# Norm, GeGLU and ternary down projection on one core: input preparation of later blocks spread over more steps, peak steps in two parts, GpSimd's long sums in short pieces

## The chip, the cores and the metric

One core of one Trainium2 chip runs the whole program. The metric is the device time of one execution in microseconds, taken as the median of several executions. Times inside the trace are microseconds from the start of the span of one profiled execution.

## What is computed

```
scale = cond @ norm_w.T + 1.0
ms = jnp.mean(x * x, axis=-1, keepdims=True)
h = x * (scale[:, None, :] * jax.lax.rsqrt(ms + EPS))
u = h @ up_w.T
val, gate = jnp.split(u, 2, axis=-1)
h = val * jax.nn.gelu(gate, approximate=False)
hq = act_quant(h)          # a row's values times 127 / row peak, rounded
wq = weight_quant(down_w)  # -1, 0 or 1, times one scale
y = hq @ wq.T
return y + x
```

x has 4 x 1024 rows of 512; up_w is 4096 x 512, down_w 512 x 2048, all float32. Float32 products are made of three float16 ones (high by high, low by high, high by low part).

## The kernel before

The 4096 rows are cut into 8 blocks of 512 tokens (b = 0 to 7), and the 2048 hidden columns into 16 tiles of 128 (j = 0 to 15). One step n = 16 b + j makes one tile of hidden values for one block. There is no scheduler: every engine has a program written out by hand, a loop over n whose body tests j against numbers, and the engines keep pace by semaphores. An engine does its own list strictly in order.

From block 2 on, a step of the up projection is a Strassen-like scheme with seven products of half tiles. On TensorE, step n runs `first_pair(n)` (12 matmuls), `third(n-1)` (6), `gates(n-1)` (12), `second(n)` (6) and `fourth(n-1)` (6). Between them stand small jobs of the other engines:

- ScalarE: `copies(n)` (lines 926 and 929) takes both halves of the first pair out of PSUM, and `second(n)` waits for it; then `absolute(n-2)` (949) and `gelu(n-1)` (942), then the step's extras.
- VectorE: `hidden(n-2)` (1317), `second_val(n-1)` (1305, which `fourth(n-1)` waits for), in steps 3 to 10 two `quantized` tiles of the block before (1398), `peak_of(n-2)` (1330), `residual` where there is one (1412), `seed_gate(n)` (1300, which `third(n)` waits for), then the step's extras.

The extras prepare block b + 1 while block b is multiplied: `norm` (1266, four per block) scales the input tile xt by the row factors; `difference` makes the sums of the scheme (XT1 into ta, XT2 into tb, XT3 in place, XN4 into ta); ScalarE's `high` (984) rounds each of seven operands to float16, and VectorE's `low` (1295) makes what is left. The row factors come from ScalarE's squares and VectorE's `rsqrt` (12 tiny instructions, lines 1239 to 1253); SyncE stores them in HBM and loads them again spread over all partitions (`store_rs`, `load_rs`), and ScalarE's `order_rs` (972) turns them into the order that `norm` reads.

For blocks 2 to 6 the row peaks are found on VectorE in the block after: `turn_peaks` (1337, 1339) at step 1 and `spread_peaks` (1347 to 1365) at step 2; the `quantized` tiles from step 3 on need its last instruction. The down projection of blocks 2 to 6 is also made of seven products, with sums on GpSimd: `down_terms` once, after step 38 (1154 to 1159), `sum_tokens` per pair of tiles (1170 to 1173), and `sum_last` (1180) after the first products of a pair of row groups, at steps 11 and 15. `row_dequant` (1388) prepares the factors for the output.

Of the kernel before, what the change touches and what calls it, by code (L numbers as in the profile page):

```python
# [8 lines left out]
ALU = mybir.AluOpType  # L9
# [36 lines left out]
def bass_cond_norm_geglu_bitlinear(  # L46
# [86 lines left out]


    V_FIRST = 2

    def h_home(b, j):
        return J + j if j < 2 and b % 2 == 1 else j
# [30 lines left out]
    with ExitStack() as ctx:  # L169
# [207 lines left out]
            return {1: 6, 2: J - 1}.get(c, (c - 1) * J)  # L377

        def rsqrt_at(c):
            return {1: 5, 2: 14, 3: J + 14, 4: 2 * J + 13}.get(c, (c - 2) * J + 11)  # L380

        def rs_away(c):

            return 1 if c == RS_DRAM else 2

        def squares_at(c, i):
            return {1: 1, 2: 9, 3: J - 1, 4: 2 * J + 9}.get(c, (c - 2) * J + 6) + i

        def xs_tile(c, i):

# [244 lines left out]
        def _(pe):  # L635
# [159 lines left out]
            def d_pair(b, p):  # L795

                x = d_index(b)
                if x == 0 and p == 0:
                    pe.wait_ge(dt_step, 4)
# [12 lines left out]

            def d_gates(b, p):
                d_product(d_high(0), q_parts[:, :, 1, 0, p, :], d_b[:, :, 1, 0, :])
                pe.wait_ge(ds4_ready, 2 * d_index(b) + p + 1)
# [106 lines left out]
        def _(act):  # L922
# [105 lines left out]
            for n in range(NJ + 2):  # L1028
# [24 lines left out]
                    if n == SUM_AT[k]:  # L1053
                        sum_high(k)
                if 1 <= b < NB - 1:
                    if j == 2:
                        high(b + 1, XB11)
                        high(b + 1, XT1)
                    if j == (2 if b < 3 else 5):
                        high(b + 1, XT2)  # L1060
                    if j == (2 if b < 3 else 8):
                        high(b + 1, XT3)
                    if j == (3 if b < 3 else 9):
                        high(b + 1, XB21)
                        high(b + 1, XB22)
                    if j == (3 if b < 3 else 11):
                        high(b + 1, XN4)
# [14 lines left out]
        def _(pool):  # L1082
# [66 lines left out]

            def down_terms():  # L1150

                b11, b12, b21, b22 = [d_b[:, :, i // 2, i % 2, :] for i in range(4)]
                pool.wait_ge(ws_ready, J)
                pool.tensor_tensor(d_t[:, 0], b12, b11, ALU.subtract, saturate=False).then_inc(dt_step, 1)
                pool.wait_ge(dt_step, 1)
                pool.tensor_tensor(d_t[:, 1], b22, d_t[:, 0], ALU.subtract, saturate=False).then_inc(dt_step, 1)
                pool.tensor_tensor(d_t[:, 2], b22, b12, ALU.subtract, saturate=False).then_inc(dt_step, 1)
                pool.wait_ge(dt_step, 2)
                pool.tensor_tensor(d_t[:, 3], b21, d_t[:, 1], ALU.subtract, saturate=False).then_inc(dt_step, 1)

            def sum_tokens(b, k):

# [12 lines left out]
            def sum_last(b, p):  # L1175

                x = d_index(b)
                pool.wait_ge(dp_ready, 2 * x + p + 1)
                pool.wait_ge(ds_step, 3 * NK * (x + 1))
                pool.tensor_tensor(q_parts[:, :, 0, 0, p, :], q_parts[:, :, 1, 0, p, :], d_s2[:, p],  # L1180
                                   ALU.subtract).then_inc(ds4_ready, 1)

            down_terms()
            for b in D_SEVEN:
# [6 lines left out]
        def _(dve):  # L1191
# [150 lines left out]
            def spread_peaks(b):  # L1342
# [15 lines left out]
                dve.tensor_scalar(scale_all[0:Q, :], row_inv, QMAX * STEP16, None, ALU.mult).then_inc(peak_step, 1)  # L1358
                dve.wait_ge(peak_step, base + 8)
# [3 lines left out]
                dve.wait_ge(xn_ready, min(b + 3, NB) * KT)  # L1363
# [89 lines left out]
            for n in range(NJ + 2):  # L1453
# [69 lines left out]
                if 1 <= b < NB - 1:  # L1523
                    if j == (0 if b == 1 else 1):
                        for kt in range(KT):
                            norm(b + 1, kt)
# [5 lines left out]
                if 1 <= b < NB - 1:  # L1532
                    if j == 2:
                        difference(b + 1, XT1)
                    if j == (2 if b < 3 else 4):
                        difference(b + 1, XT2)
                        low(b + 1, XB11)
                    if j == (2 if b < 3 else 7):
                        difference(b + 1, XT3)
                        low(b + 1, XT1)  # L1540
                    if j == (2 if b < 3 else 10):
                        difference(b + 1, XN4)
                    if j == 15:
                        for k in (XT2, XT3, XB21, XB22, XN4):
                            low(b + 1, k)
                for c in range(1, NB):
                    if n == rsqrt_at(c):
# [53 lines left out]
```

## Time and profile before

| | |
|---|---|
| time, median of 3 runs | 748.75 us (748.67 to 749.0) |
| profiled execution, its own time | 745.14 us |
| its span | 743.3 us |
| TensorE busy | 726.3 us, 98% of the span |
| VectorE busy | 548.1 us, 74% |
| ScalarE busy | 343.7 us, 46% |
| GpSimd busy | 236.3 us, 32% |
| share of TensorE in the chain that ended last | 89% |
| granted TensorE clock | 1.00 |

A share of busy time is an average over the span. A matmul's length in the trace is modelled and overlaps the next one, so the distance from one start to the next is what says how fast TensorE goes.

### The profile page before, as it was taken

Reading aid. Unit: us, or ns where it says so; the run is one execution under the profiler, and the core shown is the slowest. Engines: PE = TensorE matmul, PEld = TensorE weight load, DVE = VectorE, ACT = ScalarE, POOL = GpSimd, SP = SyncE. Lnnn points to the kernel's source line nnn. Section 1 sums busy time; section 2 is a strip of 40 time slices with the busy share of each in tenths; the row PEclk is TensorE's granted clock in tenths of the full one; section 3 lists DMA queues with packets and bytes.
Section 4 is the critical chain, followed back from the end, with each engine's and each line's share of the span. In section 5 each row is a group of like instructions: output and inputs, shape, how many; then the busy total and the mean of one; then the engine's idle time right before and its main releaser. Section 6 shows DMA issues by size and latency. Waiting matters only on the chain.

```text
span 743.3 us, 14907 instructions
## 1 busy us (share of the span) xinstructions
PE 726.3 (98%) x5722; PEld 557.9 (75%) x5722; DVE 548.1 (74%) x1024; ACT 343.7 (46%) x680; POOL 236.3 (32%) x286
## 2 busy tenths in 40 slices
PE   6999999999999999999999999899998999999998
PEld 6544444444688887888888888788887888888874
DVE  5567777975989666886689857897579955687357
ACT  5789766543365533463325534355334443334330
POOL 1211477876325300452105511154012530033100
PEclk9999999999999999999999999999999999999999
DMA  8877583847645454442545325353253324273202
GB/s 327 299 267 240 182 285 118 280 164 250 221 138 145 148 187 123 155 143 76 171 134 165 121 89 188 104 185 100 83 195 122 111 80 127 81 236 102 74 29 85
DMA packets 44567, 117.63 MB, mean 158 GB/s; under 512 B 5584, under 2 KB 5840, under 8 KB 43344
## 3 DMA queue, kind: packets, MB, share of 16 engines
q1 hardware_dynamic: 44496, 116.68, 47.9%
q8 instruction: 45, 0.74, 0.4%
q14 instruction: 26, 0.21, 0.1%
HBM read 99.88 MB, written 16.79 MB: 157 GB/s over the span
## 4 chain that ended last, share of the span: by engine, by line
PE 89%; DVE 5%; issue 3%; ACT 1%; DMA 1%; POOL 0%; DVEq 0%; SPq 0%; POOLq 0%
PE ps_v L649 13%; PE ps_v L651 13%; PE ps_v L650 13%; PE ps_y L785 6%; PE ps_g L651 5%; PE ps_g L649 5%; PE ps_g L650 5%; PE ps_y L778 5%; PE ps_v L667 4%; PE ps_g L667 4%; PE ps_v L669 4%; PE ps_g L669 4%; PE ps_v L668 4%; PE ps_g L668 4%; PE ps_v L907 1%
## 5 line engine op out<-in xcount | busy, mean ns | idle before, releaser
L649 PE MATMUL ps_v<-x_hi,w_hi 128*128 128x256 f16 x968 | 263.9, 273 | 7.7 <-ACT p L929 6.3
L650 PE MATMUL ps_v<-x_lo,w_hi 128*128 128x256 f16 x968 | 263.8, 273 | 0.0
L651 PE MATMUL ps_v<-x_hi,w_lo 128*128 128x256 f16 x968 | 263.8, 273 | 0.0
L926 ACT COPY ps_g<-ps_v 128x256 f32<-128x256 f32 x96 | 34.3, 357 | 185.6 <-PE ps_v L651 185.6
L949 ACT ACTIVATE g<-h 128x512 f32<-128x512 f32 x128 | 81.2, 634 | 72.0 <-DVE h L1317 72.0
L942 ACT ACTIVATE g<-ps_g,w_unscale 128x512 f32<-128x512 f32 x128 | 87.1, 681 | 58.1 <-PE ps_g L651 53.6
L649 PEld LDWEIGHTS ps_v<-x_hi,w_hi 128*128 128x128 f16 x968 | 94.7, 98 | 21.2 <-ACT p L929 7.1
L1170 POOL TENSOR_TENSOR sums<-q 128x256 f16<-128x256 f16 (+1 forms) x40 | 40.0, 1001 | 214.9 <-DVE q L1398 214.9
L649 PE MATMUL ps_g<-x_hi,w_hi 128*128 128x256 f16 x392 | 106.8, 273 | 0.1
L650 PE MATMUL ps_g<-x_lo,w_hi 128*128 128x256 f16 x392 | 106.8, 273 | 0.0
L651 PE MATMUL ps_g<-x_hi,w_lo 128*128 128x256 f16 x392 | 106.8, 273 | 0.0
L1330 DVE TENSOR_TENSOR h_max<-g,h_max 128x512 f32<-128x512 f32 x120 | 88.7, 739 | 20.7 <-ACT g L949 16.7
L650 PEld LDWEIGHTS ps_v<-x_lo,w_hi 128*128 128x128 f16 x968 | 94.7, 98 | 11.6
L651 PEld LDWEIGHTS ps_v<-x_hi,w_lo 128*128 128x128 f16 x968 | 94.7, 98 | 11.0
L1305 DVE TENSOR_TENSOR ps_v<-ps_v,p 128x256 f32<-128x256 f32 x96 | 41.1, 428 | 78.5 <-PE ps_v L651 78.2
L1317 DVE SCALAR_TENSOR_TENSOR h<-ps_v,h_unscale,g 128x512 f32<-128x512 f32 x128 | 95.1, 743 | 4.3 <-PE ps_v L669 1.4
L1398 DVE TENSOR_TENSOR q<-h,ps_m 128x512 f16<-128x512 f32 x112 | 71.3, 676 | 0.0
L1300 DVE TENSOR_TENSOR ps_g<-ps_v,p 128x256 f32<-128x256 f32 x96 | 41.0, 427 | 35.7 <-PE ps_v L651 35.5
L1180 POOL TENSOR_TENSOR q<-q,sums 128x1024 f16<-128x1024 f16 x9 | 20.1, 2229 | 113.0 <-PE ps_y L785 113.0
L667 PE MATMUL ps_g<-x_hi,w_hi 128*128 128x512 f16 x124 | 47.0, 379 | 0.0
L668 PE MATMUL ps_g<-x_lo,w_hi 128*128 128x512 f16 x124 | 47.0, 379 | 0.0
L669 PE MATMUL ps_g<-x_hi,w_lo 128*128 128x512 f16 x124 | 47.0, 379 | 0.0
(153 smaller groups left out, 1161.9 us busy)
## 6 DMA issues: line engine op xcount, KB each, us to landing
w_lo<-w_lo_dram SPq DMA_DIRECT2D x96, 448.0 KB, 3.2
q<-in_up_t_dram SPq DMA_DIRECT2D x16, 512.0 KB, 5.4
xt<-in_x_cols_dram SPq DMA_DIRECT2D x8, 1024.0 KB, 5.0
res<-in_x_rows_dram SPq DMA_DIRECT2D x26, 256.0 KB, 4.4
out_dram<-res SPq DMA_DIRECT2D x26, 256.0 KB, 4.1
xs<-in_x_rows_dram SPq DMA_DIRECT2D x22, 256.0 KB, 3.9
w_lo_dram<-w_lo SPq DMA_DIRECT2D x16, 256.0 KB, 4.7
dw<-in_down_t_dram SPq DMA_DIRECT2D x8, 512.0 KB, 6.5
```

The costliest lines, as they stand in the source:

```text
L649: pe.matmul(to, w_hi[:, wh:wh + P], hi, start=start and kt == 0, stop=False, skip_group_check=True)
L650: pe.matmul(to, w_hi[:, wh:wh + P], lo, start=False, stop=False, skip_group_check=True)
L651: last = pe.matmul(to, w_lo[:, wl:wl + P], hi, start=False, stop=(kt == 1), skip_group_check=True)
L667: pe.matmul(bank, w_hi[:, wh:wh + P], hi, start=start and kt == 0, stop=False)
L668: pe.matmul(bank, w_hi[:, wh:wh + P], lo, start=False, stop=False)
L669: last = pe.matmul(bank, w_lo[:, wl:wl + P], hi, start=False, stop=not start and kt == 1)
L785: last = pe.matmul(to, left[:, k, :], right[:, k, :], start=start and k == 0, stop=k == NK - 1, skip_group_check=True)
L942: act.activation(g[:, n % 3, :], ps_g[:, n % NG, :], ACT.Gelu, scale=w_unscale[:, n % J:n % J + 1]).then_inc(g_ready, 1)
L949: act.activation(g[:, n % 3, :], h[:, at:at + TB], ACT.Abs).then_inc(h_abs_ready, 1)
L1317: dve.scalar_tensor_tensor(out=h[:, at:at + TB], in0=ps_v[:, n % NV, :], scalar=h_unscale[:, j:j + 1], in1=g[:, n % 3, :], op0=ALU.mult, o ...
L1330: dve.tensor_tensor(h_max[:], g[:, n % 3, :], h_max[:], ALU.max).then_inc(h_max_ready, 1)
L1398: dve.tensor_tensor(to[:, j * TB:(j + 1) * TB], h[:, at:at + TB], ps_m[:], ALU.mult).then_inc(q_ready, 1)
```

## The change

Inputs of blocks 4 to 7 (made during blocks 3 to 6) are prepared on a new timetable; blocks 2 and 3 keep theirs. The four `norm` go from step 1 to steps 3, 4, 6, 7, one each. `difference` goes from steps 2, 4, 7, 10 to 5, 8, 11, 11. `high` goes from steps 2, 2, 5, 8, 9, 9, 11 to 5, 6, 9, 12, 12, 12, 12, and `low` from 4, 7 and five of them in step 15 to 9, 10, 12, 13, 13, 14, 15. `rsqrt` of blocks 5 to 7 goes from step 11 to 14 (for block 4 from 13 to 14), and the store, load and `order_rs` behind it come 3 steps later (2 for block 4), so that `order_rs` falls on step 2. The squares of blocks 5 to 7 come 3 steps later too. `spread_peaks` is cut in two: its first seven instructions, `gather_peaks`, follow `turn_peaks` in step 1, and the last four stay in step 2. `row_dequant` of blocks 2 to 6 goes from step 5 to 11. `down_terms` is made in 8 parts (32 instructions of 256 columns in place of 4 of 2048), and each `sum_last` in 4 (256 columns in place of 1024). TensorE's list of instructions is the same, with the counts that it waits for changed.

```diff
+    NORM_AT = (3, 4, 6, 7)
+    T_AT = {XT1: 5, XT2: 8, XT3: 11, XN4: 11}
+    HIGH_AT = {XB11: 5, XT1: 6, XT2: 9, XT3: 12, XB21: 12, XB22: 12, XN4: 12}
+    LOW_AT = {XB11: 9, XT1: 10, XT2: 12, XT3: 13, XB21: 13, XB22: 14, XN4: 15}
...
         def rsqrt_at(c):
-            return {1: 5, 2: 14, 3: J + 14, 4: 2 * J + 13}.get(c, (c - 2) * J + 11)
+            return {1: 5, 2: 14, 3: J + 14}.get(c, (c - 2) * J + 14)
...
         def squares_at(c, i):
-            return {1: 1, 2: 9, 3: J - 1, 4: 2 * J + 9}.get(c, (c - 2) * J + 6) + i
+            return {1: 1, 2: 9, 3: J - 1}.get(c, (c - 2) * J + 9) + i
...
-                pool.tensor_tensor(d_t[:, 0], b12, b11, ALU.subtract, saturate=False).then_inc(dt_step, 1)
...
+                for k in range(NK):
+                    part = slice(k, k + 1)
+                    b11, b12, b21, b22 = [d_b[:, part, i // 2, i % 2, :] for i in range(4)]
+                    t1, t2, t3, t4 = [d_t[:, i, part] for i in range(4)]
+                    pool.tensor_tensor(t1, b12, b11, ALU.subtract, saturate=False).then_inc(dt_step, 1)
...
-                pool.tensor_tensor(q_parts[:, :, 0, 0, p, :], q_parts[:, :, 1, 0, p, :], d_s2[:, p],
-                                   ALU.subtract).then_inc(ds4_ready, 1)
+                for k in range(0, NK, 2):
+                    pool.tensor_tensor(q_parts[:, k:k + 2, 0, 0, p, :], q_parts[:, k:k + 2, 1, 0, p, :], d_s2[:, p, k:k + 2],
+                                       ALU.subtract).then_inc(ds4_ready, 1)
...
+                if 3 <= b < NB - 1 and j in NORM_AT:
+                    norm(b + 1, NORM_AT.index(j))
...
-                if 1 <= b < NB and j == 5:
+                if 1 <= b < NB and j == (11 if by_vector(b - 1) else 5):
                     row_dequant(b - 1)
...
+                if 1 <= b < NB and j == 1 and by_vector(b - 1):
+                    gather_peaks(b - 1)
...
+                if 3 <= b < NB - 1:
+                    for k in (XT1, XT2, XT3, XN4):
+                        if j == T_AT[k]:
+                            difference(b + 1, k)
+                    for k in made(b + 1):
+                        if j == LOW_AT[k]:
                             low(b + 1, k)
```

VectorE at step 2 of block 4, from `seed_gate` on, before. The 32x16 instructions are `spread_peaks`, `ta<-xt` is the difference XT1, and `h<-ps_v` opens step 3:

```order
L1300 TENSOR_TENSOR ps_g<-ps_v,p 128x256
L1412 SCALAR_TENSOR_TENSOR res<-ps_y,dequant,res 128x512
L1347 COPY tb<-tb 32x16 x3
L1350 TENSOR_REDUCE row_peak<-tb 32x16
L1353 TENSOR_SCALAR row_peak<-row_peak 32x16
L1355 RECIPROCAL tb<-row_peak 32x16
L1358 TENSOR_SCALAR tb<-tb 32x16
L1361 COPY tb<-tb 32x16 x3
L1365 STREAM_TRANSPOSE ps_m<-tb 128x512
L1275 TENSOR_TENSOR ta<-xt 128x512
L1317 SCALAR_TENSOR_TENSOR h<-ps_v,h_unscale,g 128x512
L1305 TENSOR_TENSOR ps_v<-ps_v,p 128x256
```

The same place after:

```order
L1302 TENSOR_TENSOR ps_g<-ps_v,p 128x256
L1418 SCALAR_TENSOR_TENSOR res<-ps_y,dequant,res 128x512
L1367 COPY tb<-tb 32x16 x3
L1371 STREAM_TRANSPOSE ps_m<-tb 128x512
L1319 SCALAR_TENSOR_TENSOR h<-ps_v,h_unscale,g 128x512
L1307 TENSOR_TENSOR ps_v<-ps_v,p 128x256
```

Seven of the eleven small instructions have gone to step 1, where four `norm` have left, and the difference to step 5.

ScalarE at step 2 of block 4 before: `copies`, `absolute`, `gelu`, two `high` (the second reads ta), and step 3:

```order
L926 COPY ps_g<-ps_v 128x256
L929 COPY p<-ps_v 128x256
L949 ACTIVATE g<-h 128x512
L942 ACTIVATE g<-ps_g,w_unscale 128x512
L984 CAST x_hi<-xt 128x512
L984 CAST x_hi<-ta 128x512
L926 COPY ps_g<-ps_v 128x256
L929 COPY p<-ps_v 128x256
```

And after:

```order
L933 COPY ps_g<-ps_v 128x256
L936 COPY p<-ps_v 128x256
L956 ACTIVATE g<-h 128x512
L949 ACTIVATE g<-ps_g,w_unscale 128x512
L979 COPY xs<-xs 128x512
L933 COPY ps_g<-ps_v 128x256
L936 COPY p<-ps_v 128x256
```

Both `high` have left step 2, and `order_rs` (`xs<-xs`) has come.

VectorE from `seed_gate` of step 14 of block 3, before: the second residual, then step 15 at once:

```order
L1300 TENSOR_TENSOR ps_g<-ps_v,p 128x256
L1412 SCALAR_TENSOR_TENSOR res<-ps_y,dequant,res 128x512
L1317 SCALAR_TENSOR_TENSOR h<-ps_v,h_unscale,g 128x512
L1305 TENSOR_TENSOR ps_v<-ps_v,p 128x256
L1330 TENSOR_TENSOR h_max<-g,h_max 128x512
```

After, with a `low` and the `rsqrt` (12 instructions of 128x4; the middle ones are left out) in front of step 15:

```order
L1302 TENSOR_TENSOR ps_g<-ps_v,p 128x256
L1418 SCALAR_TENSOR_TENSOR res<-ps_y,dequant,res 128x512
L1297 TENSOR_TENSOR x_lo<-xt,x_hi 128x512
L1241 TENSOR_SCALAR ms<-sumsq 128x4
...
L1255 SCALAR_TENSOR_TENSOR rs<-rs_t,rs 128x4
L1319 SCALAR_TENSOR_TENSOR h<-ps_v,h_unscale,g 128x512
L1307 TENSOR_TENSOR ps_v<-ps_v,p 128x256
```

Thirteen instructions more now stand between `seed_gate(62)` and `second_val(62)`; the same holds in blocks 4 and 5.

## Rows read from the trace of the kernel before

**Rows 1.** The page, parts 1 and 4: busy time, and the chain's shares

```profile
PE 726.3 (98%) x5722; PEld 557.9 (75%) x5722; DVE 548.1 (74%) x1024; ACT 343.7 (46%) x680; POOL 236.3 (32%) x286
...
PE 89%; DVE 5%; issue 3%; ACT 1%; DMA 1%; POOL 0%; DVEq 0%; SPq 0%; POOLq 0%
```

**Rows 2.** Waits, whole span: waiter <- releaser: us in total, times, longest

```profile
PE ps_v L649 <- ACT p L929: 6.3, 3, 2.1
...
PE ps_v L649 <- DVE ps_g L1300: 0.7, 1, 0.7
...
PE ps_v L649 <- DVE ps_v L1305: 0.6, 1, 0.6
```

**Rows 3.** Timeline of TensorE, 388.1 to 390.9: start, length, instruction, [idle before <- releaser]

```profile
388.25 0.27 PE L651 MATMUL ps_g<-x_hi,w_lo 128*128 128x256 f16 x1
390.61 0.28 PE L649 MATMUL ps_v<-x_hi,w_hi 128*128 128x256 f16 x1 [2.09 <-ACT p L929]
```

**Rows 4.** Timeline of ScalarE, 381 to 392.5

```profile
389.36 0.62 ACT L984 CAST x_hi<-ta 128x512 f16<-128x512 f32 x1 [4.79 <-DVE ta L1275]
...
390.19 0.37 ACT L929 COPY p<-ps_v 128x256 f32<-128x256 f32 x1
```

**Rows 5.** Timeline of VectorE, 376 to 391.5

```profile
378.10 2.73 DVE L1266 SCALAR_TENSOR_TENSOR xt<-xt,cs,xs 128x512 f32<-128x512 f32 x4
...
385.75 0.56 DVE L1347 COPY tb<-tb 32x16 f32<-32x16 f32 x3
...
387.29 0.56 DVE L1361 COPY tb<-tb 32x16 f32<-32x16 f32 x3
...
388.64 0.69 DVE L1275 TENSOR_TENSOR ta<-xt 128x512 f32<-128x512 f32 x1
```

**Rows 6.** Timelines of TensorE, GpSimd and VectorE, 228 to 249

```profile
236.55 0.28 PE L649 MATMUL ps_v<-x_hi,w_hi 128*128 128x256 f16 x1 [0.73 <-DVE ps_g L1300]
...
231.77 3.83 POOL L1154 TENSOR_TENSOR dw<-dw 128x2048 fp8e4<-128x2048 fp8e4 x1 [22.06 <-DVE xs L1226]
...
233.79 2.36 DVE L1330 TENSOR_TENSOR h_max<-g,h_max 128x512 f32<-128x512 f32 x1
236.07 0.42 DVE L1300 TENSOR_TENSOR ps_g<-ps_v,p 128x256 f32<-128x256 f32 x1
```

**Rows 7.** Timelines of TensorE and VectorE in the last block, 652 to 654

```profile
653.33 0.28 PE L649 MATMUL ps_v<-x_hi,w_hi 128*128 128x256 f16 x1 [0.61 <-DVE ps_v L1305]
...
652.85 0.42 DVE L1305 TENSOR_TENSOR ps_v<-ps_v,p 128x256 f32<-128x256 f32 x1
```

**Rows 8.** Timelines of VectorE and TensorE, steps 14 and 15 of block 3

```profile
360.52 0.74 DVE L1412 SCALAR_TENSOR_TENSOR res<-ps_y,dequant,res 128x512 f32<-128x512 f32 x1
361.18 0.74 DVE L1317 SCALAR_TENSOR_TENSOR h<-ps_v,h_unscale,g 128x512 f32<-128x512 f32 x1
362.80 0.43 DVE L1305 TENSOR_TENSOR ps_v<-ps_v,p 128x256 f32<-128x256 f32 x1 [0.88 <-PE ps_v L651]
...
364.56 0.27 PE L649 MATMUL ps_v<-x_hi,w_hi 128*128 128x256 f16 x1
```

**Rows 9.** Timeline of VectorE, 262 to 265: first of the `rsqrt`, and what follows it

```profile
262.65 0.16 DVE L1239 TENSOR_SCALAR ms<-sumsq 128x4 f32<-128x4 f32 x1
...
264.94 0.75 DVE L1317 SCALAR_TENSOR_TENSOR h<-ps_v,h_unscale,g 128x512 f32<-128x512 f32 x1
```

**Rows 10.** Timeline of VectorE, 308 to 311, extras of step 4, block 3

```profile
308.72 0.82 DVE L1281 TENSOR_TENSOR tb<-xt,ta 128x512 f32<-128x512 f32 x1
309.46 1.15 DVE L1295 TENSOR_TENSOR x_lo<-xt,x_hi 128x512 f16<-128x512 f32 x1
```

**Rows 11.** Groups of GpSimd by line and form: count | busy, mean ns | idle before

```profile
L1170 POOL TENSOR_TENSOR sums<-q 128x256 f16<-128x256 f16 x32 | 33.6, 1050 | 174.3 <-DVE q L1398 174.3
...
L1180 POOL TENSOR_TENSOR q<-q,sums 128x1024 f16<-128x1024 f16 x9 | 20.1, 2229 | 113.0 <-PE ps_y L785 113.0
```

**Rows 12.** DMA issues by line: count, size, median us from issue to landing

```profile
xs<-rs_dram SPq DMA_DIRECT2D x4, 256.0 KB, 3.7
```

More of the change, by code:

```diff
@@ L135, in bass_cond_norm_geglu_bitlinear @@
     V_FIRST = 2
+    NORM_AT = (3, 4, 6, 7)
+    T_AT = {XT1: 5, XT2: 8, XT3: 11, XN4: 11}
+    HIGH_AT = {XB11: 5, XT1: 6, XT2: 9, XT3: 12, XB21: 12, XB22: 12, XN4: 12}
+    LOW_AT = {XB11: 9, XT1: 10, XT2: 12, XT3: 13, XB21: 13, XB22: 14, XN4: 15}
+    HIGH_EARLY = {XB11: 2, XT1: 2, XT2: 2, XT3: 2, XB21: 3, XB22: 3, XN4: 3}
     def h_home(b, j):
@@ L379, in rsqrt_at @@
         def rsqrt_at(c):
-            return {1: 5, 2: 14, 3: J + 14, 4: 2 * J + 13}.get(c, (c - 2) * J + 11)
+            return {1: 5, 2: 14, 3: J + 14}.get(c, (c - 2) * J + 14)
         def rs_away(c):
-            return 1 if c == RS_DRAM else 2
+            return 2
         def squares_at(c, i):
-            return {1: 1, 2: 9, 3: J - 1, 4: 2 * J + 9}.get(c, (c - 2) * J + 6) + i
+            return {1: 1, 2: 9, 3: J - 1}.get(c, (c - 2) * J + 9) + i
         def xs_tile(c, i):
@@ L798, in d_pair @@
                 if x == 0 and p == 0:
-                    pe.wait_ge(dt_step, 4)
+                    pe.wait_ge(dt_step, 4 * NK)
                 pe.wait_ge(ds_step, 3 * NK * (x + 1))
@@ L814, in d_gates @@
                 d_product(d_high(0), q_parts[:, :, 1, 0, p, :], d_b[:, :, 1, 0, :])
[L815 removed]
+                pe.wait_ge(ds4_ready, (2 * d_index(b) + p + 1) * NK // 2)
                 d_product(d_high(1), q_parts[:, :, 0, 0, p, :], d_b[:, :, 1, 1, :]).then_inc(y_ready, 1)
@@ L1055, in _ @@
                 if 1 <= b < NB - 1:
[L1056 to L1067, printed above, removed]
+                    for k in made(b + 1):
+                        if j == (HIGH_EARLY if b < 3 else HIGH_AT)[k]:
+                            high(b + 1, k)
                 for c in range(1, NB):
@@ L1150, in down_terms @@
             def down_terms():
-                b11, b12, b21, b22 = [d_b[:, :, i // 2, i % 2, :] for i in range(4)]
                 pool.wait_ge(ws_ready, J)
-                pool.tensor_tensor(d_t[:, 0], b12, b11, ALU.subtract, saturate=False).then_inc(dt_step, 1)
[L1155 to L1159, printed above, removed]
+                for k in range(NK):
[3 more added lines that the diff above has]
+                    pool.tensor_tensor(t1, b12, b11, ALU.subtract, saturate=False).then_inc(dt_step, 1)
+                    pool.wait_ge(dt_step, 4 * k + 1)
+                    pool.tensor_tensor(t2, b22, t1, ALU.subtract, saturate=False).then_inc(dt_step, 1)
+                    pool.tensor_tensor(t3, b22, b12, ALU.subtract, saturate=False).then_inc(dt_step, 1)
+                    pool.wait_ge(dt_step, 4 * k + 2)
+                    pool.tensor_tensor(t4, b21, t2, ALU.subtract, saturate=False).then_inc(dt_step, 1)
             def sum_tokens(b, k):
@@ L1340, in turn_peaks, with gather_peaks @@
                                   ALU.max).then_inc(peak_step, 1)
-            def spread_peaks(b):
+            def gather_peaks(b):
                 base = (b - V_FIRST) * PEAK_STEPS
@@ L1358, in spread_peaks @@
                 dve.tensor_scalar(scale_all[0:Q, :], row_inv, QMAX * STEP16, None, ALU.mult).then_inc(peak_step, 1)
+            def spread_peaks(b):
+                base = (b - V_FIRST) * PEAK_STEPS
                 dve.wait_ge(peak_step, base + 8)
@@ L1362, in spread_peaks @@
                 dve.wait_ge(peak_step, base + 11)
-                dve.wait_ge(xn_ready, min(b + 3, NB) * KT)
+                dve.wait_ge(xn_ready, RS_DRAM * KT)
                 dve.wait_ge(q_ready, b * J)
@@ L1520, in _ @@
                     dve.reciprocal(d_scale[:], d_mean[:]).then_inc(d_scale_ready, 1)
-                if 1 <= b < NB and j == 5:
+                if 1 <= b < NB and j == (11 if by_vector(b - 1) else 5):
                     row_dequant(b - 1)
[L1523 to L1526, printed above, removed]
+                if 1 <= b < 3 and j == b - 1:
+                    for kt in range(KT):
+                        norm(b + 1, kt)
                 for k in range(J):
@@ L1531, in _ @@
                     turn_peaks(b - 1)
-                if 1 <= b < NB - 1:
+                if 1 <= b < NB and j == 1 and by_vector(b - 1):
+                    gather_peaks(b - 1)
+                if 1 <= b < 3:
                     if j == 2:
                         difference(b + 1, XT1)
-                    if j == (2 if b < 3 else 4):
                         difference(b + 1, XT2)
                         low(b + 1, XB11)
-                    if j == (2 if b < 3 else 7):
                         difference(b + 1, XT3)
                         low(b + 1, XT1)
-                    if j == (2 if b < 3 else 10):
                         difference(b + 1, XN4)
@@ L1544, in _ @@
                         for k in (XT2, XT3, XB21, XB22, XN4):
+                            low(b + 1, k)
+                if 3 <= b < NB - 1:
+                    for k in (XT1, XT2, XT3, XN4):
+                        if j == T_AT[k]:
+                            difference(b + 1, k)
+                    for k in made(b + 1):
+                        if j == LOW_AT[k]:
                             low(b + 1, k)
```

## The prediction

> **What bounds the kernel now.** I began with the page's busy times and the shares of the chain: TensorE is busy 98% of the span and holds 89% of the chain [rows 1]. It is the bound, and its list of matmuls does not change. So the change can be worth only the time in which TensorE stands still, and I went to the waits of the whole span for it. Apart from the start, three kinds are left [rows 2]: three waits on `copies` of ScalarE, 6.3 us; one on `seed_gate`, 0.7 us; one on `second_val`, 0.6 us. Then I read the timeline at one of each kind, to see what was late and behind what it stood.
>
> A wait in the trace is shorter than what it costs, since a matmul's end is modelled. In [rows 3] the starts are 2.36 us apart where two neighbours are 0.11 apart, so 2.25 us are lost, and the row says 2.09. The difference, 0.16, I add to every wait.
>
> - First kind, in step 3 of blocks 4, 5 and 6. ScalarE stood 4.79 us in front of the `high` that reads ta [rows 4], and `copies` of the next step is behind it on the same engine; its second half ends at 390.56, and TensorE goes on at 390.61 [rows 3]. What ScalarE waited for is the difference XT1, the last thing that VectorE does in step 2, at 388.64, behind all of `spread_peaks`, which starts at 385.75 [rows 5]. Cost 3 x 2.25 = 6.75 us.
> - Second kind, in step 8 of block 2. `peak_of` took 2.36 us and ended just after GpSimd's first long sum of `down_terms` (231.77 + 3.83 = 235.60); `seed_gate` behind it started at 236.07 and TensorE went on at 236.55 [rows 6]. Cost 0.73 + 0.16 = 0.89 us.
> - Third kind, in step 3 of the last block. There is no difference XT1 there, but `spread_peaks` alone makes `second_val` start at 652.85, and TensorE waits for it until 653.33 [rows 7]. Cost 0.61 + 0.16 = 0.77 us.
>
> Together 8.41 us, all that can be won outside the start and the end.
>
> **Step 2, blocks 4 to 6: gain 6.75.** ScalarE no longer reads ta in step 2: the difference comes in step 5 and its `high` in step 6, a step later, so the 4.79 us go. In its place stands `order_rs`, which needs the loaded row factors (see the rivals). VectorE's own path there gets shorter too. Step 1 loses the four norms, 2.65 us from 378.10 to the next instruction, and gets the seven instructions of `gather_peaks`, 387.29 - 385.75 = 1.54 us [rows 5]; step 2 loses these 1.54 us and the difference, 0.61. Step 3 opens 2.1 us earlier on VectorE, so I see nothing else late behind the stall. I take the full 6.75.
>
> **Step 3 of the last block: gain 0.77.** `second_val` comes 1.54 us earlier in step 3, at 651.31, ends at 651.73, and TensorE would need it at 653.33 - 0.77 = 652.56 [rows 7]. Step 1 gets 1.54 us heavier there, with no norms to leave it; in block 4 that step carried 2.65 us of norms in the same place without a wait of TensorE [rows 2, 5].
>
> **Step 8 of block 2: gain 0.89.** With `down_terms` in 32 pieces, `peak_of` is held up by one piece at most. A piece has 256 columns; the nearest rows are 1.05 us for 256 columns behind a wait, and 2.23 / 4 = 0.56 us from the rate of the 1024-column sum [rows 11]. With 0.56, `peak_of` ends by 233.79 + 0.56 + 0.69 = 235.04 instead of 236.15, and nothing is late (TensorE was free to go on 0.89 before 236.55, at 235.66). With 1.05, `seed_gate` ends near 235.9 and 0.2 to 0.3 us stay. I take the first, since most pieces follow another directly. All 32 pieces take 18 to 34 us in place of 16.6, so they end by 266; the first product that reads them is in step 11 of block 3, and that block's step 4 is only at 308.72 [rows 10]. `sum_last` in four pieces (at most 4 x 1.05 = 4.2 us in place of 2.23) is needed only two steps later. The longer GpSimd work costs nothing on the path.
>
> **Steps 3 to 13: cost 0.** Steps 3 to 10 each carry two quantized tiles and now at most one thing more: a norm (2.65 / 4 = 0.66), a difference (up to 0.82) or a `low` (up to 1.15 beside GpSimd's sums). Step 4 of block 3 carries a difference and a `low` together, 1.82 us from 308.72 to 310.54, with the same two tiles, and TensorE does not wait there [rows 2, 10]. What hides them is VectorE's idle time in front of `second_val`; without that cover they would cost their length. Steps 11 to 13 have no quantized tiles and two or three such instructions; ScalarE's four `high` in step 12 (about 2.1 us) are less than the 2.5 us that it has free there (it stood 4.79 and cost 2.25) [rows 3, 4].
>
> **Step 14, blocks 3 to 5: cost 1.95.** This is what the new timetable breaks. In step 14 VectorE already has the two residuals of the down projection, the second at 360.52, right after a `seed_gate` that cannot come earlier; then step 15 opens at 361.18 and `second_val` runs at 362.80 [rows 8]. Now `low` of XB22 (about 0.60 start to start, as the difference of the same size in [rows 5]) and the whole `rsqrt` stand between: an `rsqrt` takes 264.94 - 262.65 = 2.29 us [rows 9]. So `hidden` starts at 361.18 + 0.60 + 2.29 = 364.07, `second_val` 0.66 later at 364.73, and it ends at 365.16. TensorE's `fourth(62)`, which waits for it, starts at 364.56 today [rows 8]. With 0.05 us to pass the signal on (390.56 to 390.61 in [rows 3, 4]) the loss is 365.21 - 364.56 = 0.65 us, in blocks 3, 4 and 5; block 6 has no `rsqrt` to make. For block 4's factors `rsqrt` falls in step 14 of block 2, which has no residuals, and costs nothing. Bounds: 0 if the chain is 0.65 shorter than I read, 1.2 a block if GpSimd's pieces touch it.
>
> **Sum.** -6.75 - 0.77 - 0.89 + 1.95 = -6.46 us. The profiled execution took 745.14 us (span 743.3) and should take 738.7. The median of the runs is 748.75, 3.6 above the profiled one; I carry the difference over: 742.3 us, 0.9% less. A change within 0.2% (1.5 us) is about what cannot be told from none here.
>
> **The rivals.**
>
> - The `rsqrt` in step 14 costs nothing, because VectorE gets there earlier than I read. For it: 0.65 us is a small difference of long sums. Against: `seed_gate` there follows TensorE and cannot move. 740.3 us; chance 0.14.
> - New waits in steps 3 to 13. The norms move from step 1, where GpSimd is idle, to steps in which it sums tokens. If VectorE and GpSimd hold each other up, as `peak_of` shows, each norm can last one GpSimd instruction longer, 1.05 us [rows 11]: 1.71 us, still under the 1.82 of step 4, but now in steps 3 and 4, and 6 and 7, in a row. If one wait of 1.05 comes through per block, 4 x 1.05 = 4.2: 746.5 us. Chance of this or of smaller waits like it, 0.16. The Trainium skill (SBUF — State Buffer, section "SBUF: two separate sides") says that VectorE and GpSimd share a port pair as an exclusive lock for a whole instruction, and that a VectorE instruction with two SBUF inputs wants it against a GpSimd one that reads SBUF. By that rule every such norm is held up; `peak_of` in [rows 6] behaves like it, and no norm of this form meets GpSimd in the trace of before.
> - The stalls stay or move: something else in steps 2 and 3 is as late. Within 0.2% of 748.75; chance 0.04. Against it: ScalarE's wait names one cause, 4.79 us long.
> - Slower: the row factors arrive late. `order_rs` is now in step 2 with `copies` behind it, one step after `load_rs`. The load takes 3.7 us [rows 12]; a step of 42 matmuls at 0.11 is 4.6 us, and `order_rs` stands where the waiting `high` stood, nearly 3 us into the step, so it has some 7.4 us, and 2.5 more before TensorE waits. Beyond 9.9 us every microsecond costs four (blocks 3 to 6). The point from which it decides is 9.9 + 6.46 / 4 = 11.5 us, three times the usual; at 12.5 us the kernel takes 742.3 + 4 x 2.6 = 752.7. Chance 0.04.
>
> **How the numbers follow.** My forecast has 0.62: 742.3, with 741.2 to 743.6 of its own (the `down_terms` wait kept in part, the `rsqrt` term between 0.3 and 1.0 a block). The range reaches down to the case without the `rsqrt` stall and up into the small new waits: 740.1 to 744.3, which leaves out the long waits, no effect and slower. Faster by over 0.2%: 0.62 + 0.14 + 0.16 = 0.92; the same 0.04; slower 0.04.
>
> **What would show it.** In the changed kernel's waits the three of 2.1 us on ScalarE's `copies` should be gone, and so should that on `second_val` near the start of the last block. Three new waits of TensorE on `second_val`, near 0.5 us as the row gives it, should stand in step 15 of blocks 3, 4 and 5. `peak_of` should never exceed about 1.3 us near `down_terms`. The forecast is wrong if ScalarE's `order_rs` shows a wait for the load, if norms of 1 us and more appear with waits of TensorE behind them, or if TensorE's idle time in the middle of the span is not about 2 us.

## The result: 1.4% faster, more than half as much again as forecast

The kernel after takes 738.49 us (median of 4 runs, 738.23 to 739.27), the kernel before 748.71 us beside it (4 runs, 748.67 to 749.0): 10.2 us less, a ratio of 0.9864 with a 95% interval of 0.9847 to 0.9882. The forecast was 742.3 us, in a range of 740.1 to 744.3. The time lies below the range. The kernel after was taken once more later, beside other runs of the kernel before: 738.92 us against 748.07, 9.15 us less (ratio 0.9882, 0.9869 to 0.9896).

The profiled execution tells another story. It took 738.35 us where the sum had 738.7, with a span of 736.6 us. So the sum made against the profiled execution of before (745.14 us) was right to 0.4 us. The two profiled executions are 6.8 us apart and the medians 10.2, so 3.4 us of the gain are not in the two traces at all. Finding those is most of what follows.

The page of the kernel after, its parts 1 and 4, answers to [rows 1]:

```profile
PE 726.2 (99%) x5722; PEld 558.4 (76%) x5722; DVE 530.1 (72%) x1024; ACT 344.0 (47%) x680; POOL 247.1 (34%) x341
...
PE 95%; DVE 2%; issue 1%; DMA 0%; POOL 0%; ACT 0%; DVEq 0%; SPq 0%; POOLq 0%
```

TensorE does the same work in less time, and now holds 95% of the chain. Its waits in the middle of the span, from the view of all waits, have shrunk to one kind (compare [rows 2]):

```profile
PE ps_v L656 <- DVE ps_v L1307: 1.5, 3, 0.5
```

They are the three that the forecast put in step 15 of blocks 3, 4 and 5. The timelines of VectorE and TensorE there:

```profile
359.48 0.74 DVE L1418 SCALAR_TENSOR_TENSOR res<-ps_y,dequant,res 128x512 f32<-128x512 f32 x1
360.13 0.68 DVE L1297 TENSOR_TENSOR x_lo<-xt,x_hi 128x512 f16<-128x512 f32 x1
360.73 0.16 DVE L1241 TENSOR_SCALAR ms<-sumsq 128x4 f32<-128x4 f32 x1
...
363.03 0.75 DVE L1319 SCALAR_TENSOR_TENSOR h<-ps_v,h_unscale,g 128x512 f32<-128x512 f32 x1
363.70 0.42 DVE L1307 TENSOR_TENSOR ps_v<-ps_v,p 128x256 f32<-128x256 f32 x1
```

```profile
363.41 0.27 PE L658 MATMUL ps_v<-x_hi,w_lo 128*128 128x256 f16 x1
364.18 0.28 PE L656 MATMUL ps_v<-x_hi,w_hi 128*128 128x256 f16 x1 [0.49 <-DVE ps_v L1307]
```

The `low` takes its 0.60 us, the `rsqrt` 2.30 us, and TensorE's starts are 0.77 us apart where 0.11 is usual: 0.66 us lost, against 0.65 in the forecast.

In step 2 and 3 of block 4, where [rows 3], [rows 4] and [rows 5] had the long wait, the timelines of ScalarE and VectorE now read:

```profile
383.31 1.11 ACT L979 COPY xs<-xs 128x512 f32<-128x512 f32 x1
386.22 0.36 ACT L933 COPY ps_g<-ps_v 128x256 f32<-128x256 f32 x1 [1.79 <-PE ps_v L658]
```

```profile
385.37 0.56 DVE L1367 COPY tb<-tb 32x16 f32<-32x16 f32 x3
385.97 0.73 DVE L1371 STREAM_TRANSPOSE ps_m<-tb 128x512 f32<-128x512 f32 x1
386.73 0.75 DVE L1319 SCALAR_TENSOR_TENSOR h<-ps_v,h_unscale,g 128x512 f32<-128x512 f32 x1
...
389.85 0.82 DVE L1268 SCALAR_TENSOR_TENSOR xt<-xt,cs,xs 128x512 f32<-128x512 f32 x1
```

`order_rs` starts with no idle time in front, so the factors had long arrived; `copies` then waits 1.79 us for TensorE and not the other way round.

### The profile page after: what moved, and what is told of

It is laid out like the page before. It is cut to its first block, busy times and chain, and to the rows that moved or that the text cites. A ratio compares the mean times of both kernels' runs of the same rounds, so it can differ in the third digit from the quotient of the medians.

```text
span 736.6 us, 14962 instructions
## 1 busy us (share of the span) xinstructions
PE 726.2 (99%) x5722; PEld 558.4 (76%) x5722; DVE 530.1 (72%) x1024; ACT 344.0 (47%) x680; POOL 247.1 (34%) x341
## 4 chain that ended last, share of the span: by engine, by line
PE 95%; DVE 2%; issue 1%; DMA 0%; POOL 0%; ACT 0%; DVEq 0%; SPq 0%; POOLq 0%
PE ps_v L656 14%; PE ps_v L658 14%; PE ps_v L657 14%; PE ps_y L792 7%; PE ps_g L658 6%; PE ps_g L657 6%; PE ps_g L656 6%; PE ps_y L785 5%; PE ps_v L674 4%; PE ps_g L674 4%; PE ps_g L676 4%; PE ps_v L676 4%; PE ps_v L675 4%; PE ps_g L675 4%; PE ps_v L914 1%
## 5 line engine op out<-in xcount | busy, mean ns | idle before, releaser
L1182 POOL TENSOR_TENSOR q<-q,sums 128x256 f16<-128x256 f16 x36 | 23.1, 672 | 113.2 <-PE ps_y L792 113.2
```

## The experiments

**The kernel before once more.** No edit, to see where its ordinary executions differ from the profiled one.

> The kernel before, unchanged. Its profiled execution took 745.14 us, its ordinary ones 748.7, and the kernel after shows no such difference (738.35 and 738.5), so 3.6 us of the gain have no place in the two traces. Theory A: each stop of 2.25 us lets TensorE's granted clock fall in most executions, though not in the profiled one; then the executions of 748.7 show a mean granted clock near 0.995 (3.6 us at half speed beyond what full speed would need, 3.6/748), and an execution of 745.1 shows 1.0. Theory B: the 3.6 us lie elsewhere (the start, a transfer); then the clock reads 1.0 at 748.7 too. Theory C: the profiled execution was of another day or chip; then a new one takes 748.7 as well with the waits unchanged.

This time the profiled execution took 748.6 us, with the same stops in it (6.3 us on `copies` in three waits, 0.7, 0.6) and a mean granted clock of 0.995. The view by windows of 1 us, after the second of the three stops, shows where. Columns: stretch, its length, busy time and instructions of TensorE, its weight loads, VectorE, ScalarE and GpSimd, then granted clock, DMA share, GB/s.

```profile
476.00:477.00 1.00, 0.57 (x6) 0.26 (x3) 0.97 (x2) 0.00 (x0) 0.00 (x0) 1.00 1.00 384
477.00:478.00 1.00, 0.00 (x0) 0.00 (x0) 1.00 (x3) 0.59 (x2) 0.00 (x0) 1.00 0.65 250
478.00:479.00 1.00, 0.34 (x4) 0.31 (x5) 1.00 (x4) 1.00 (x4) 0.00 (x0) 1.00 0.01 2
479.00:480.00 1.00, 1.00 (x9) 0.77 (x7) 1.00 (x2) 0.70 (x2) 0.36 (x1) 0.68 0.00 0
480.00:481.00 1.00, 1.00 (x7) 0.67 (x6) 0.70 (x3) 0.00 (x0) 0.92 (x2) 0.50 0.00 0
481.00:482.00 1.00, 1.00 (x6) 0.72 (x5) 0.55 (x1) 0.00 (x0) 1.00 (x2) 0.50 0.43 57
482.00:483.00 1.00, 1.00 (x8) 0.72 (x6) 0.00 (x0) 0.00 (x0) 0.06 (x1) 0.61 0.81 290
483.00:484.00 1.00, 1.00 (x12) 0.90 (x10) 0.19 (x1) 0.85 (x3) 0.00 (x0) 1.00 0.35 128
```

The stop ends at 478.66; from 479.3 the clock is at 0.50, the lower of its two levels (1.2 GHz), until about 482.8, and 6 to 7 matmuls start per microsecond in place of 12. The profiled execution whose rows stand ahead of the prediction has the same stop and a clock of 1.00 in these windows:

```profile
479.00:480.00 1.00, 1.00 (x12) 0.89 (x11) 1.00 (x3) 0.50 (x1) 0.56 (x1) 1.00 0.00 0
480.00:481.00 1.00, 1.00 (x12) 0.90 (x10) 0.95 (x2) 0.00 (x0) 0.92 (x2) 1.00 0.07 22
```

In TensorE's timeline of the new execution the starts go from 0.11 to 0.21 us apart:

```profile
479.10 0.27 PE L650 MATMUL ps_v<-x_lo,w_hi 128*128 128x256 f16 x1
479.21 0.27 PE L651 MATMUL ps_v<-x_hi,w_lo 128*128 128x256 f16 x1
...
480.13 0.42 PE L650 MATMUL ps_v<-x_lo,w_hi 128*128 128x256 f16 x1
480.34 0.42 PE L651 MATMUL ps_v<-x_hi,w_lo 128*128 128x256 f16 x1
```

Some 3.4 us at half speed are 1.7 us of work not done. By the starts of the stops, the way from the second to the third is 89.52 us here (476.295 to 565.811) and 87.84 us in the execution read first (476.100 to 563.944), and the way from the third to the wait of the last block 90.12 against 88.50: a fall after the second and after the third stop, 1.6 to 1.7 us each, none after the first. The fall at the third stop begins just when TensorE goes on again (568.17), since the mean of this window is already 0.56, 0.12 us at full clock and the rest at half:

```profile
568.00:569.00 1.00, 0.83 (x5) 0.57 (x6) 1.00 (x3) 1.00 (x3) 0.00 (x0) 0.56 0.00 0
```

One such fall, 3.4 us at half the clock, takes 0.0023 off a mean over 745 us. The 63 executions of the kernel before (12 here, 51 beside the experiments) fall into three groups by their mean granted clock:

| mean granted clock | executions | time, us |
|---|---|---|
| 1.0 | 1 | 744.93 |
| 0.997 to 0.998 | 31 | 746.60 to 748.16 |
| 0.995 | 31 | 748.34 to 749.42 |

No fall, one fall, two falls. The execution read before the forecast (745.14 us, clock 1.00) was one of the rare ones without a fall, and the four that make the median of 748.71 all lie in the range of the last group. Theory A holds, and theory B is out, since the clock is not 1.0 at 748. Theory C foresaw a new profiled execution of 748.7 us with the same waits, and that came; but it has no place for the steps of 1.7 us or for the clock, and the execution of 744.93 us at a clock of 1.0 ran among 16 others of 746.7 to 749.1 us. A mean of 0.999, which some executions below show, is no fall of this kind: in the two traces that have it the low clock stands in the last 1.0 to 1.3 us of the span, when TensorE has no work left.

**One edit: ScalarE's `high` of XT1 a step later,** in blocks 3 to 6.

```diff
                         high(b + 1, XB11)
+                    if j == (2 if b < 3 else 3):
                         high(b + 1, XT1)
```

> The kernel before with one edit: in blocks 3 to 6 ScalarE's rounding of XT1 comes in step 3 and not in step 2. Nothing else moves. If the wait for the difference XT1 is all that stops TensorE in step 3, the three waits of 2.1 us vanish and the profiled execution falls by 6.75 us to 738.4; the waits of 0.7 and 0.6 us stay. Theory A (clock): ordinary executions fall by 6.75 + 3.6 to about 738.4 and show a clock of 1.0. Theory B: they fall by 6.75 only, to 742.0. A rival for the mechanism, that VectorE itself is as late as ScalarE (second_val behind spread_peaks, as in the last block with 0.77 a block), gives 740.7 profiled.

743.33 us (743.28 to 743.37), ratio 0.9941 (0.9928 to 0.9954), clock 0.999 to 1.0 in all five executions. The waits of TensorE:

```profile
PE ps_v L649 <- DVE ps_v L1306: 4.2, 4, 1.2
...
PE ps_v L649 <- DVE ps_g L1301: 0.7, 1, 0.7
```

ScalarE's wait is gone and another has taken its place. The timeline of VectorE in the same step:

```profile
388.23 0.73 DVE L1366 STREAM_TRANSPOSE ps_m<-tb 128x512 f32<-128x512 f32 x1
388.99 0.69 DVE L1276 TENSOR_TENSOR ta<-xt 128x512 f32<-128x512 f32 x1
389.60 0.74 DVE L1318 SCALAR_TENSOR_TENSOR h<-ps_v,h_unscale,g 128x512 f32<-128x512 f32 x1
390.26 0.42 DVE L1306 TENSOR_TENSOR ps_v<-ps_v,p 128x256 f32<-128x256 f32 x1
```

`second_val` was right behind: the 0.77 us of the last block [rows 7] and 0.60 for the difference in front of it make the 1.37 us lost at each of these stops (0.15 more follow). Of 2.25 us, ScalarE's wait alone was worth 0.7. This was the rival, with a bigger stop than it named, since the expectation left the difference out. The median is 4.3 us under the 747.61 us of the kernel before beside it, and 2.2 of these are in the stops. The executions show a second thing: stops of 1.37 us, 15 of them in five executions, and no fall.

**The change without its `rsqrt` in step 14.**

```diff
-            return {1: 5, 2: 14, 3: J + 14}.get(c, (c - 2) * J + 14)
+            return {1: 5, 2: 14, 3: J + 14}.get(c, (c - 2) * J + 13)
...
-            return 2
+            return 3
```

> The kernel after with the rsqrt of blocks 4 to 7 in step 13 in place of 14, and its store, load and reordering left where they are. In step 13 no residuals stand before it. By the sum of the prediction the three waits on second_val in step 15 (0.49 us each in the trace, 0.65 us lost each) vanish and nothing new comes: 738.49 - 1.96 = 736.5 us. The rival, that the rsqrt makes the d_fourth or second_val of step 13 late as it did in step 14, gives no change (738.5) with the waits one step earlier.

736.9 us (736.44 to 737.36), ratio to before 0.9853 (0.9836 to 0.987). The view of waits has none of TensorE after the first 25 us of the span. It ran again beside the kernel after, on one chip.

> The kernel rsqrt13, unchanged, beside the kernel after on the same chip: 1.96 us less than it (three times 0.65 us), 736.4 to 736.9 us. If the gain of the first run was scatter of the start of the program, where TensorE once waited 1.3 us for ScalarE, the difference is another.

> The kernel after, unchanged, on the same chip as rsqrt13_again: 738.4 us, clock 1.0, three waits on second_val of 0.49 us.

736.57 us (736.29 to 736.79) and 738.92 us (738.55 to 739.49): 2.35 us apart, where the three stops make 1.96. The trace of the kernel after has the three waits again (1.5 us in all), that of rsqrt13 none; the other 0.4 us fits the scatter of the start of the program, where TensorE waited 0.5 us for ScalarE at about 11 us in the profiled execution of rsqrt13 and 0.9 us in that of the kernel after. It is the fastest version of this study.

**The change with GpSimd's long sums.** `down_terms` and `sum_last` as before, all else as after. The lines of `sum_last`:

```diff
-                for k in range(0, NK, 2):
-                    pool.tensor_tensor(q_parts[:, k:k + 2, 0, 0, p, :], q_parts[:, k:k + 2, 1, 0, p, :], d_s2[:, p, k:k + 2],
-                                       ALU.subtract).then_inc(ds4_ready, 1)
+                pool.tensor_tensor(q_parts[:, :, 0, 0, p, :], q_parts[:, :, 1, 0, p, :], d_s2[:, p],
+                                   ALU.subtract).then_inc(ds4_ready, 1)
...
```

> The kernel after with GpSimd's down_terms and sum_last in long pieces again, as before. If the pieces are what removed the wait in step 8 of block 2, it comes back and costs 0.89 us: 739.4. If sum_last in long pieces also holds up VectorE in steps 12 and 0 where the new timetable has work, up to 2.3 us each on one instruction, new waits would add to that, up to 1 us a block: 742. The rival, that the timetable alone already removed it, gives 738.5.

739.43 us (739.34 to 739.67), ratio 0.9889 (0.9875 to 0.9904), 0.94 us above the kernel after's first median and 0.51 above its second. The wait in step 8 of block 2 is back, and nothing else:

```profile
PE ps_v L656 <- DVE ps_v L1303: 1.5, 3, 0.5
...
PE ps_v L656 <- DVE ps_g L1298: 0.7, 1, 0.7
```

So the pieces of `down_terms` are worth the 0.89 us of the sum, and those of `sum_last` nothing that a wait of TensorE shows. With pieces, the timelines of GpSimd and VectorE at that place in the kernel after answer to [rows 6]:

```profile
232.95 0.64 POOL L1158 TENSOR_TENSOR dw<-dw 128x256 fp8e4<-128x256 fp8e4 x1
233.55 0.64 POOL L1160 TENSOR_TENSOR dw<-dw 128x256 fp8e4<-128x256 fp8e4 x1
234.14 1.09 POOL L1155 TENSOR_TENSOR dw<-dw 128x256 fp8e4<-128x256 fp8e4 x1
```

```profile
233.66 1.08 DVE L1332 TENSOR_TENSOR h_max<-g,h_max 128x512 f32<-128x512 f32 x1
234.66 0.42 DVE L1302 TENSOR_TENSOR ps_g<-ps_v,p 128x256 f32<-128x256 f32 x1
```

A piece is 0.64 us, and `peak_of` is 1.08 us long in place of 2.36. It starts at 233.66, beside the piece that began at 233.55, and ends 0.55 us after that piece does (234.74 after 234.19); in [rows 6] it ended 0.55 us after the long sum (236.15 after 235.60). The next piece is 0.45 us longer than the others.

**The pieces alone,** in the kernel before: the lines of `down_terms` and `sum_last` in the change's diff and nothing else of it.

> The kernel before with GpSimd's down_terms and sum_last in short pieces and nothing else. In the trace the one wait on seed_gate in step 8 of block 2 goes (0.90 us), the three stops of 2.25 us stay, and so do the falls of the clock (none, one or two a run at 1.6 us): the executions lie in groups near 744.3, 745.8 and 747.7, the median 0.9 under that of the kernel before on the same chip. If pieces cost VectorE more than they free (36 more instructions on the shared way to memory), no change or slower.

746.14 us (744.34 to 748.84, 11 runs) beside 748.07, ratio 0.9986 (0.9973 to 0.9999). The wait on `seed_gate` is gone from the trace, the three stops stay. (The pages count 55 GpSimd instructions more for the pieces, 341 against 286, not the 36 of the expectation.) One execution has a clock of 1.0 (744.34 us), six have 0.997 or 0.998 (745.67 to 746.75), four 0.995 (747.39 to 748.84): the groups of the kernel before, 0.6 us lower for the single ones without a fall and 0.8 to 1.0 us by the means of the other two. The median itself says little here, since it depends on how many of the runs fell how often.

**The change with the peak steps in one part.** The call of `gather_peaks` goes from step 1 to step 2, in front of `spread_peaks`.

```diff
                 if 1 <= b < NB and j == 2 and by_vector(b - 1):
+                    gather_peaks(b - 1)
                     spread_peaks(b - 1)
...
-                if 1 <= b < NB and j == 1 and by_vector(b - 1):
-                    gather_peaks(b - 1)
```

> The kernel after with the peak steps in one part again, all eleven in step 2. By the sum VectorE then opens step 3 of blocks 4 to 6 at the time of the last block before, since the difference XT1 (0.6 us) is gone and gather_peaks (1.54 us) is back: TensorE waits 0.77 us for second_val and 0.15 behind it in blocks 4, 5, 6 and 7, 3.7 us in all: 742.2 us, with the clock at 1.0 (stops under 1 us). If the timetable alone were enough: 739.4, the wait of the last block only.

742.4 us (742.34 to 742.66), ratio 0.9927 (0.9913 to 0.9941), clock 0.999 to 1.0. TensorE waits seven times on `second_val`:

```profile
PE ps_v L656 <- DVE ps_v L1307: 3.9, 7, 0.6
```

Three are those of step 15, four are new, in step 3 of blocks 4 to 7, 0.77 us lost each and 0.15 behind it: 3.7 us by the trace, 3.5 to 3.9 us by the medians of the two runs of the kernel after. The timetable alone is not enough; both halves of the change are needed to clear step 3.

**The peak steps in two parts alone,** in the kernel before. The function is cut in two as in the change, and the first part is called in step 1:

```diff
...
                     turn_peaks(b - 1)
+                    gather_peaks(b - 1)
```

> The kernel before with the peak steps in two parts and nothing else. The norms stay in step 1 and the difference XT1 at the end of step 2, at the same time as before, so the three stops of 2.25 us stay and so do the falls of the clock; the 0.92 us of the last block go; VectorE in step 1 of blocks 4 to 6 reaches second_val about 0.3 us too late. Profiled with no fall: 745.1; the median in the same range as the kernel before, 745 to 748. If the split alone freed the stall, the time would fall to about 739.

744.23 us (743.9 to 744.56), ratio 0.9951 (0.9938 to 0.9963). The waits of TensorE:

```profile
PE ps_v L649 <- ACT p L929: 4.9, 3, 1.6
...
PE ps_v L649 <- DVE ps_g L1300: 0.7, 1, 0.7
...
PE ps_v L649 <- DVE ps_v L1305: 0.6, 3, 0.2
```

The expectation missed this one: not 745 to 748 with falls, but no fall at all, clock 1.0 in five of five. The stop in step 3 is 1.79 us and no longer 2.25, because 0.37 us are lost a step earlier, and with them TensorE comes to the same point later. The stops add up to nearly the same (2.16 against 2.25 a block), and with the last block's gone all stops together fell by 1.2 us (8.57 to 7.39). Yet the median is 4.25 us under the 748.48 us of the kernel before beside it: the other 3 us are the falls. Whether it is the size of the longest stop or the other stop in front of it that matters, this run alone does not tell.

**Stops put into a kernel that has none.** In rsqrt13, ScalarE does `order_rs` several times over, with the same result, so that `copies` comes late. In stops5 there are four more in front of the one that was there, five in all; stops6 has one more again (5 in place of each 4), six in all.

```diff
+                for k in range(4):
+                    act.copy(xs[:, 1, :].rearrange("p (i q) -> p i q", i=TT),
+                             xs[:, 0, :].rearrange("p (q i) -> p i q", i=TT)).then_inc(again, 1)
+                    act.wait_ge(again, 4 * (c - RS_DRAM) + k + 1)
```

> The kernel rsqrt13 (736.9 us, no wait of TensorE in the middle of the span), with ScalarE's order_rs done five times over in step 2 (the same result each time), so that copies of step 3 comes late. One order_rs is 1.11 us; five with their signals take about 5.8 us, copies starts 1.7 us later than TensorE can take, in blocks 4, 5 and 6 (block 3 has a long step there): three stops of about 1.7 us, 5.2 us. If each stop costs its length alone: 742.1. Clock theory: stops of 1.37 us (high_late) left the clock at 1.0 in five executions, stops of 2.25 us did not; this size lies between, and if the clock falls here a fall costs 1.6 us more: up to 746.9, and the executions differ by steps of 1.6.

Three stops of 1.67 to 1.68 us. 741.87 us (741.54 to 742.52), clock 0.999 to 1.0: 5.0 us over rsqrt13's 736.9, their length alone and no fall in 15 stops.

> As stops5 with six order_rs: three stops of about 2.9 us, longer than those of the kernel before, 8.7 us, 0.3 more in block 3. If a stop costs its length alone: 745.9, all executions alike. If a stop of more than 2 us is what lets the clock fall to half, whatever the program around it: two to three falls of 1.6 us more, 749.1 to 750.7, a mean granted clock of 0.993 to 0.996, and executions that differ by 1.6 us.

Three stops of 2.80 to 2.82 us, and one of 0.2. 746.51 us (745.26 to 748.56, 12 runs). Five executions have a clock of 1.0 (745.26 to 746.04), six 0.997 or 0.998 (746.41 to 747.92), one 0.995 (748.56): eight falls in 36 stops. The windows of the profiled execution (the one of 748.56 us) after its first long stop, which ends at 390.6:

```profile
391.00:392.00 1.00, 1.00 (x11) 0.89 (x9) 0.88 (x2) 0.66 (x2) 0.00 (x0) 0.90 0.00 0
392.00:393.00 1.00, 1.00 (x7) 0.70 (x5) 1.00 (x3) 0.00 (x0) 0.00 (x0) 0.50 0.00 0
393.00:394.00 1.00, 1.00 (x7) 0.69 (x6) 0.47 (x1) 0.00 (x0) 0.00 (x0) 0.50 0.71 151
394.00:395.00 1.00, 1.00 (x6) 0.74 (x5) 0.00 (x0) 0.14 (x1) 0.00 (x0) 0.50 0.77 308
395.00:396.00 1.00, 1.00 (x10) 0.84 (x8) 0.23 (x1) 1.00 (x3) 0.00 (x0) 0.90 0.00 0
```

Its second fall begins at 480.54, 0.14 us before TensorE goes on after the second stop. The fall of the clock comes back when the stops come back, in a program that shows none otherwise, neither without stops nor with the five `order_rs` of stops5. Long stops are the cause. But the expectation was too high: two to three falls a run were foreseen, and 0.7 came, fewer than the 1.5 of the kernel before, whose stops are shorter. So length is not all.

The last of these puts the six `order_rs` into one block only (against stops6):

```diff
-                for k in range(5):
+                for k in range(5 if c == 6 else 0):
...
-                    act.wait_ge(again, 5 * (c - RS_DRAM) + k + 1)
+                    act.wait_ge(again, k + 1)
```

> The kernel rsqrt13 with the six order_rs in one block alone (block 5), so one stop of 2.8 us in place of three. A stop alone costs its length: 739.7. If one stop in itself can let the clock fall, some executions are 1.6 us longer, 741.3, with a mean granted clock of 0.998; of stops6's 12 executions 7 had a clock of 0.998 or less, 8 or 9 falls in 36 stops, so about one execution in four. If a fall needs several stops in a row of blocks, none falls.

740.31 us (739.42 to 740.76, 4 runs), ratio 0.9899 (0.9885 to 0.9913). Three executions have a clock of 1.0, one (740.76 us) has 0.997. That one is a fall by its clock, but only 1.3 us above the fastest, inside what the start scatters; with four executions this is a hint that one stop is enough, and no more.

## Why the prediction was right in the trace and wrong in the time

**The terms, one by one.** Start to start, the trace of before loses 2.25, 2.25, 2.25, 0.90, 0.77 and, behind the last, 0.15 us in the middle of its span, 8.57 us; that of after loses 0.66, 0.65 and 0.65, 1.96 us. That is 6.6 us less; the forecast had 6.46, and the profiled executions are 6.8 apart. The start is in this too: the matmul that starts at 53.18 us before starts at 53.05 after, and between 53.05 and 54.41 in all the traces. That the sum met the trace to 0.4 us is therefore in part luck; that the big terms are right one by one is not.

- Step 2 of blocks 4 to 6, 6.75 us: right, and right for the reason given. ScalarE's wait named the first obstacle only; high_late shows `second_val` 0.7 us behind it. The forecast counted VectorE's relief (step 3 to open 2.1 us earlier) in the same term. It opens at 386.73 where it was 389.25, and the whole trace is 0.38 us earlier by then (`copies` of step 2 at 380.76 against 381.14): 2.1 us.
- The last block, 0.77 us: right; the 0.15 us behind it was left out. no_split puts both back.
- `down_terms`, 0.89 us: right, by long_sums (0.89 in the trace, 0.94 and 0.51 by the medians). The piece was taken as 0.56 us and is 0.64.
- Steps 3 to 13 at no cost: right, the view has no wait of TensorE there.
- Step 14, 1.95 us lost: right to 0.01, and confirmed by taking it out (rsqrt13).

**The step that failed** is the one behind the sum: "The median of the runs is 748.75, 3.6 above the profiled one; I carry the difference over". The 3.6 us were taken for something that belongs to every execution of either kernel. They were two falls of the granted clock, about 1.7 us each, and these hung on the very stops that the change removes. They had to be a term of the sum: -6.46 - 3.4 from 748.7 is 738.8, and 738.5 was measured. How large the carried error was is in part chance: the kernel before falls 93 times in 63 executions, 1.5 times on average, or some 2.5 us, and by their times all four beside the result had fallen twice. The profiled execution showed a clock of 1.00 throughout, so its rows could not say so; but a median 0.5% above the profiled time, where the runs agree to 0.04%, was a plain sign of something that this trace does not show. The range had only costs of the change in it, and no line for a difference that goes away with the stops.

**The rivals.** The free `rsqrt` and the late row factors are out: the three waits came, and `order_rs` never waits. The new waits in steps 3 to 13 did not come either, but their cause is partly there. The group of norms in the kernel after, by form:

```profile
L1268 DVE SCALAR_TENSOR_TENSOR xt<-xt,cs,xs 128x512 f32<-128x512 f32 x16 | 13.3, 828 | 0.0
```

They took 744 ns each in step 1, with GpSimd idle, and 828 ns now beside its sums (905 at most). The rival took each norm to be held up by one whole GpSimd instruction, 1.05 us. The rows show less to wait for, here for the norm at 389.85 (shown above, 0.82 us long) and for the one of 905 ns:

```profile
389.08 1.05 POOL L1171 TENSOR_TENSOR sums<-q 128x256 f16<-128x256 f16 x1 [19.70 <-DVE q L1404]
390.20 1.00 POOL L1173 TENSOR_TENSOR q<-q 128x256 f16<-128x256 f16 x1
```

```profile
303.44 0.67 POOL L1173 TENSOR_TENSOR q<-q 128x256 f16<-128x256 f16 x1
303.75 0.91 DVE L1268 SCALAR_TENSOR_TENSOR xt<-xt,cs,xs 128x512 f32<-128x512 f32 x1
```

When a norm starts, the GpSimd instruction beside it has only 0.27 or 0.28 us to go (0.36 for the long one), and each of the 16 norms ends 0.55 us after that instruction does, just as `peak_of` does after its own: 390.67 after 390.13, and 304.66 after 304.11. GpSimd pays too: its next instruction takes 1.00 us, where the same one took 0.67 at 303.44. The Trainium skill (SBUF — State Buffer, section "SBUF: two separate sides"), which the prediction weighed, has whichever instruction starts first keep the pair of ports to its end; the 16 norms agree with it. What the rival had too large is the rest of the instruction that a norm meets: 0.28 us, of which 0.08 show.

**What stays open.** Why a stop of 2.25 us in the kernel before let the clock fall in about half of the cases (93 falls in 63 executions with three stops each), one of 2.8 us in the altered kernel in 8 of 36, and stops of 1.4 to 1.8 us in none of 45. Every stop here is followed by the same work, but what TensorE did in the microseconds before it differs, and where a stop falls in time may matter too. For the second speak the four falls that the windows of before_again and stops6 show: they begin between 0.1 us before TensorE goes on again and 1.2 us after, and the two of one execution begin 88.75 us apart in both, though the stops end 89.51 us apart in before_again and 90.07 in stops6. No run here separates the two.

## What to carry to other kernels

When the profiled execution and the median of the runs differ by more than the runs differ among themselves, find what the difference is before carrying it over to another kernel: here it was tied to the very waits that the change removed, and was worth half as much as they. A stop of TensorE as long as those here (2.25 and 2.8 us) can cost 1.7 us beyond its length, so a few long stops can be worth more to remove than their sum in the waits; in split_only, where they became 1.79 and 0.37 us, the falls went too. And when a wait is taken away, look at what stands right behind it on the other engines: the named wait was worth 0.7 of the 2.25 us, and only the change of both engines' lists brought the rest. A chain of small dependent instructions wants a step with room in front of the next thing that TensorE needs: the `rsqrt` moved out of the step with the residuals, by one step, is worth 2 us.

## What the runs showed of the hardware that was not expected

- After or during a stop of TensorE of 2.25 us (2.8 us in stops6), the granted clock fell to 0.50 (1.2 GHz) for about 3.4 us. In the traces of before_again and stops6 the fall began between 0.1 us before the matmuls resumed and 1.2 us after; the matmuls of 256 columns start 0.21 us apart meanwhile. It happened in some executions of the same program and not in others, with the same stops in the trace. The Trainium skill (TensorE: Matmul & The Clock Gate, section "HAM oscillation — how this bites in real kernels") describes idle gaps that send a kernel back to the lower clock; the runs here agree in kind, with gaps shorter than the ones that it describes.
- A VectorE instruction with two inputs in SBUF that starts beside a GpSimd sum and is held up by it ends 0.55 us after that sum, for a long one and a short one alike (236.15 after 235.60 before, 234.74 after 234.19 after). It gets in between two GpSimd instructions that stand directly one behind the other, and the second of these is then the longer (1.09 us for 0.64).
